# Routed tiles: one semaphore update of TensorE a slot, three PSUM banks a link, stages 3, 6 and 9 slots behind the load

## What is computed

```python
xn = (xf - mu) * jax.lax.rsqrt(var + LN_EPS) * ln_scale + ln_bias
probs = jax.nn.softmax(xn @ gate_w.T, axis=-1)
tk_probs, tk_idx = jax.lax.top_k(probs, TOP_K)          # 2 of 8 experts
tk_probs = tk_probs / (jnp.sum(tk_probs, axis=-1, keepdims=True) + EPS)
out = _swiglu(xf, sWg, sWu, sWd)                        # shared expert
for e in range(NUM_EXPERTS):
    out = out + w[:, e:e + 1] * _swiglu(xf, Wg[e], Wu[e], Wd[e])
# _swiglu(x, wg, wu, wd) = jax.nn.silu(x @ wg) * (x @ wu) @ wd
```

## Time and profile before

| | |
|---|---|
| median of 3 runs | 887.57 us (887.54 to 888.57) |
| profiled execution, its span from the first to the last instruction | 935.9 us |
| TensorE busy in it | 785.4 us, 84% |
| VectorE busy | 651.4 us, 70% |
| ScalarE busy | 573.1 us, 61% |
| GpSimd busy | 569.9 us, 61% |
| mean granted TensorE clock | 0.928 |

### The profile page before, as it was taken

One profiled execution on the slowest core, in us unless ns is written; L12 is line 12 of the kernel. 1 busy time (PEld: TensorE's weight loads), 2 busy tenths in 40 slices (PEclk: granted clock), 3 DMA queues, 4 the chain that ended last, 5 costly groups with the idle time before them and its releaser, 6 DMA issues.

```text
span 935.9 us, 37055 instructions
## 1 busy us (share of the span) xinstructions
PE 785.4 (84%) x14487; PEld 614.1 (66%) x14487; DVE 651.4 (70%) x1699; ACT 573.1 (61%) x1185; POOL 569.9 (61%) x762
## 2 busy tenths in 40 slices
PE   4888997998898888989868777899988999998890
PEld 3556676766676666667655546788767777777770
DVE  2347787888988798788787777586555555556773
ACT  4478886877887788778756554443344545545440
POOL 5455554877877787778656565357155555655562
PEclk9799998989899899889987878999999999999996
DMA  8311101220221122022112005001232222225765
GB/s 242 65 49 48 48 28 36 60 64 25 68 60 34 54 60 68 20 66 60 32 53 60 25 21 157 21 12 38 66 84 78 77 74 77 76 75 174 212 186 170
DMA packets 81446, 68.39 MB, mean 73 GB/s; under 512 B 9424, under 2 KB 71515, under 8 KB 81280
## 3 DMA queue, kind: packets, MB, share of 16 engines
q1 hardware_dynamic: 70000, 47.81, 19.4%
q0 software_dynamic: 8640, 16.93, 5.4%
q10 hardware_dynamic: 2640, 1.31, 0.5%
HBM read 42.91 MB, written 24.02 MB: 72 GB/s over the span
## 4 chain that ended last, share of the span: by engine, by line
PE 41%; DVE 26%; issue 17%; ACT 8%; SPq 4%; DMA 2%; another core or an unknown queue 1%; POOL 1%; POOLq 0%; ACTq 0%; DVEq 0%
PE pair_x L886 8%; PE bank L904 7%; PE bank L501 4%; DVE mx L1510 4%; PE pair_x L677 4%; PE pair_x L587 3%; PE bank L694 3%; DVE Ex L1514 2%; ACT Am L992 2%; DVE rot L1442 2%; DVE c_hit L1606 2%; PE bank L894 1%; PE bank L623 1%; PE pair_y L894 1%
## 5 line engine op out<-in xcount | busy, mean ns | idle before, releaser
L1405 POOL DMA_INDIRECT mixed<-f_y,f_x x142 | 139.4, 982 | 129.8 <-ACT f_y L1178 81.6
L1288 POOL DMA_INDIRECT routed<-c_row,c_idx x128 | 137.1, 1071 | 104.7 <-PE bank L694 61.2
L904 PEld LDWEIGHTS bank<-Qblk,Am 128*128 128x128 f32 x568 | 79.4, 191 | 47.4 <-issue 39.8
L904 PE MATMUL bank<-Qblk,Am 128*128 x568 | 92.5, 285 | 16.4 <-DVE Am L1816 12.2
L677 PE MATMUL pair_x<-con,Ex 128*128 128x128 f32 x512 | 77.9, 302 | 20.7 <-ACT Am L992 18.4
L1178 ACT ACTIVATE f_y<-bank,f_x 128x128 f32<-128x128 f32 x142 | 52.5, 370 | 56.8 <-PE bank L904 49.5
L992 ACT ACTIVATE Am<-pair_x 128x1024 f32<-128x1024 f32 x64 | 65.1, 1016 | 36.0 <-PE pair_x L587 27.5
L1027 ACT COPY ExT<-pair_x 128x1024 f32<-128x1024 f32 x64 | 64.5, 1008 | 34.4 <-PE pair_x L677 30.1
L1173 ACT ACTIVATE qk<-pair_x 128x256 f32<-128x256 f32 x142 | 55.5, 391 | 48.2 <-PE pair_x L886 31.0
L587 PE MATMUL pair_y<-Kblk,KQ 32*64 32x256 f32 x1024 | 82.8, 437 | 0.7 <-issue 0.7
L677 PEld LDWEIGHTS pair_x<-con,Ex 128*128 128x128 f32 x512 | 64.6, 156 | 27.4 <-issue 23.9
(11 more groups left out here) (209 smaller groups left out, 2083.0 us busy)
## 6 DMA issues: line engine op xcount, KB each, us to landing
f_x<-routed SPq DMA_DIRECT2D x142, 65.0 KB
ctxD<-in_ctx SPq DMA_DIRECT2D x32, 256.0 KB
ctxP<-in_ctx SPq DMA_DIRECT2D x16, 256.0 KB
maskB<-in_mask_BxS_if SPq DMA_DIRECT2D x16, 256.0 KB
Cblk<-mixed SPq DMA_DIRECT2D x8, 512.0 KB
Kblk<-mixed SPq DMA_DIRECT2D x8, 512.0 KB
block_out<-X SPq DMA_DIRECT2D x11, 256.0 KB
mixed<-f_y,f_x POOLq DMA_INDIRECT x142
```

The source lines that it names most:

```text
L904: ins = pe.matmul(banks[F_O[n % 2]][:, 0:D], f_hT[:, u % 3, c * P:(c + 1) * P], wdn[:, bass.ds(e, 1), c, :].rearrange("p o d -> p (o d)"), ...
L1288: pool.indirect_dma_start(routed[:, :], bass.IndirectOffsetOnAxis(ap=c_idx[:, d % ROW_SLOTS, t, n:n + 1], axis=0), c_row[:, d % ROW_SLOTS, ...
L1405: pool.indirect_dma_start(mixed[:, :], bass.IndirectOffsetOnAxis(ap=f_x[:, u, D + 1:D + 2].bitcast(I32), axis=0), f_y[:, u, :], None, boun ...
```

## The change

TensorE makes one update of one semaphore, `f_slot`, with the last matmul of each slot. ScalarE and VectorE wait for it once at the start of their slot, in place of four waits for four semaphores. The up product of a tile comes 3 slots behind its transpose (was 2), its hidden transpose 6 (was 4), its down product 9 (was 6), and LAG is 9. Each kind of PSUM result but one has three banks: the transposed tile n shares its bank with the output of tile n-9, in other columns; the hidden transpose keeps two. Since ScalarE and VectorE mustn't read one bank at once, `tile_low` now waits for `tile_end` of the same slot (`f_yd`), and comes last in VectorE's slot. SBUF rings have 4 places (were 3), the load ring 18 (was 15), in another room. The mixed sums of part 0 start 3 slots later. Four semaphores of the setup are one, with the values 1 to 4.

```diff
-UNROLL = 15
+UNROLL = 18
 EARLY_SUM, SUM_EVERY = PART_FIRST[1] + UNROLL - 1, 3
+LOAD_STEPS = max(TILE_MAX, EARLY_SUM + SUM_EVERY * (EARLY - 1) + 1)
-LAG = 6
+UP_BACK, TURN_BACK, LAG = 3, 6, 9
-E_RING = 6
+E_RING = 10
+F_RING = 4
+SET_WEIGHTS, SET_GATE, SET_BIAS, SET_TABLE = 1, 2, 3, 4
-        F_UP, F_HT, F_X, F_O = (0, 1), (3, 4), (2, 6), (5, 7)
+        F_UP, F_XO, F_HT = (0, 1, 2), (4, 5, 6), (3, 7)
...
@@ SyncE
-            for n in range(UNROLL, TILE_MAX):
+            for n in range(UNROLL, LOAD_STEPS):
...
-                load_tile(n)
+                if n < TILE_MAX:
+                    load_tile(n)
...
@@ TensorE
+            def tile_T(n, t, u):
                 pe.wait_ge(f_in[u], 16 * t + 16)
-                if n >= 2:
-                    pe.wait_ge(S["f_xTl"], n - 1)
-                pe.transpose(banks[F_X[n % 2]][:, 0:P], f_x[:, u, 0:D], ident).then_inc(S["f_xT_ps"], 1)
+                if n >= 3:
+                    pe.wait_ge(S["f_xTl"], n - 2)
+                return pe.transpose(banks[F_XO[n % 3]][:, 0:P], f_x[:, u, 0:D], ident)
...
+            def tile_up(n, e):
                 pe.wait_ge(S["f_xTl"], n + 1)
-                if n >= 2:
-                    pe.wait_ge(S["f_hd"], n - 1)
+                if n >= 3:
+                    pe.wait_ge(S["f_hd"], n - 2)
...
+            def tile_down(n, e):
+                pe.wait_ge(S["f_hTd"], n + 1)
+                if n >= 3:
+                    pe.wait_ge(S["f_yd"], n - 2)
...
+            def hidden_T(n):
+                pe.wait_ge(S["f_hd"], n + 1)
+                if n >= 2:
+                    pe.wait_ge(S["f_hTd"], n - 1)
...
             def slot(t, u):
+                n = t * UNROLL + u
+                if n < TILE_MAX:
+                    ins = tile_T(n, t, u)
+                if 0 <= n - UP_BACK < TILE_MAX:
+                    ins = tile_up(n - UP_BACK, expert_of(n - UP_BACK))
+                if 0 <= n - 1 < TILE_MAX:
+                    load_expert(n - 1)
+                if 0 <= n - LAG < TILE_MAX:
+                    ins = tile_down(n - LAG, expert_of(n - LAG))
+                if 0 <= n - TURN_BACK < TILE_MAX:
+                    ins = hidden_T(n - TURN_BACK)
+                ins.then_inc(S["f_slot"], 1)
...
@@ ScalarE
             def slot(t, u):
+                act.wait_ge(S["f_slot"], n + 1)
+                if n < TILE_MAX:
+                    tile_T_evac(n)
+                if 0 <= n - UP_BACK < TILE_MAX:
+                    tile_silu(n - UP_BACK)
+                if 0 <= n - LAG < TILE_MAX:
+                    tile_end(n - LAG)
...
@@ VectorE
+            def tile_low(n):
                 dve.wait_ge(S["f_xTd"], n + 1)
+                if n >= LAG:
+                    dve.wait_ge(S["f_yd"], n - LAG + 1)
...
             def slot(t, u):
+                n = t * UNROLL + u
+                dve.wait_ge(S["f_slot"], n + 1)
+                if 0 <= n - TURN_BACK < TILE_MAX:
+                    hidden_evac(n - TURN_BACK)
+                if 0 <= n - UP_BACK < TILE_MAX:
+                    hidden(n - UP_BACK)
+                if n < TILE_MAX:
+                    tile_low(n)
```

More of the change, by code:

```diff
@@ L449, in _ @@
                     store(i - 3)
-            for i in range((TILE_MAX - 1 - EARLY_SUM) // SUM_EVERY - 2, EARLY):
+            for i in range((LOAD_STEPS - 1 - EARLY_SUM) // SUM_EVERY - 2, EARLY):
                 store(i)
@@ L898, in tile_down @@
-            def tile_down(t, u, e):
-                n = t * UNROLL + u
-                pe.wait_ge(S["f_hTd"], n + 1)
-                if n >= 2:
-                    pe.wait_ge(S["f_yd"], n - 1)
-                for c in range(CH):
-                    ins = pe.matmul(banks[F_O[n % 2]][:, 0:D], f_hT[:, u % 3, c * P:(c + 1) * P],
+                return ins
+            def tile_down(n, e):
+                pe.wait_ge(S["f_hTd"], n + 1)
+                if n >= 3:
+                    pe.wait_ge(S["f_yd"], n - 2)
+                for c in range(CH):
+                    ins = pe.matmul(banks[F_XO[n % 3]][:, P:P + D], f_hT[:, n % F_RING, c * P:(c + 1) * P],
@@ new lines, in hidden_T @@
+            def hidden_T(n):
+                pe.wait_ge(S["f_hd"], n + 1)
+                if n >= 2:
+                    pe.wait_ge(S["f_hTd"], n - 1)
+                for c in range(CH):
+                    ins = pe.transpose(banks[F_HT[n % 2]][:, c * P:(c + 1) * P],
+                                       f_h[:, n % F_RING, c * P:(c + 1) * P], ident)
+                return ins
+            def slot(t, u):
+                n = t * UNROLL + u
[10 more added lines that the diff above has]
+                ins.then_inc(S["f_slot"], 1)
@@ L1162, in _, with tile_T_evac, tile_silu, tile_end @@
             act.wait_ge(S["s_ac"], GROUPS)
[L1164 to L1184 removed]
+            def tile_T_evac(n):
+                act.copy(f_xT_hi[:, n % F_RING, :], banks[F_XO[n % 3]][:, 0:P]).then_inc(S["f_xTd"], 1)
+            def tile_silu(n):
+                act.activation(f_sg[:, n % F_RING, :], banks[F_UP[n % 3]][:, 0:INTER], ACT.Silu).then_inc(S["f_si"], 1)
+            def tile_end(n):
+                u = n % UNROLL
+                act.activation(f_y[:, u, :], banks[F_XO[n % 3]][:, P:P + D], ACT.Copy, scale=f_x[:, u, D:D + 1])\
+                    .then_inc(S["f_yd"], 1)
+            def slot(t, u):
+                n = t * UNROLL + u
+                act.wait_ge(S["f_slot"], n + 1)
[5 more added lines that the diff above has]
+                    tile_end(n - LAG)
             routed_slots(slot)
@@ L1830, in slot @@
             def slot(t, u):
-                for stage, back in ((tile_low, 0), (hidden_evac, 5), (hidden, 2)):
-                    tile = tile_of(t, u, back)
-                    if tile:
-                        stage(*tile)
-                i, rest = divmod(t * UNROLL + u - EARLY_SUM + 1, SUM_EVERY)
+                n = t * UNROLL + u
[6 more added lines that the diff above has]
+                    tile_low(n)
+                i, rest = divmod(n - EARLY_SUM + 1, SUM_EVERY)
                 if i in range(EARLY) and rest < TOP:
```

100 lines of the change are left out of this document (29 added, 71 removed).

## The result

The changed kernel takes 900.19 us (median of 4 runs, 898.75 to 903.04); the kernel before, beside it, 888.07 us (887.54 to 889.93). The ratio is 1.0133, interval 1.0091 to 1.0176: slower by 12.1 us. The forecast was 889.0, the range 855 to 891, slower by over 0.2% with a chance of 0.26.

The account below looks back on a forecast made before the run. TensorE's own work, 1.46 us a slot, was taken as the routed stage's floor, with late releases likelier than not from recording. 0 - 2.5 (start) + 3.9 (drain) = +1.4 on 887.57 gave 889.0; own range 886.6 to 891.3, 8-in-10 range 855 to 891.

Parts of the forecast that it names:

- TensorE has one more wait a slot: 0: Routed stage: hidden_T's added wait for f_hTd is for something two slots old, so it costs 0.
- The drain, +3.9: End of routed stage: nine slots behind, more scatters queue on GpSimd after the last transpose; +3.9 us, bounds +2.5 to +3.9.
- The start, -2.5: Start of routed stage: with UNROLL 18, 18 loads go ahead of the pads, shortening TensorE's stop; -2.5 us, ends -1.5 and -3.5.
- the clock: After the stop for the pads: a longer stop can drop TensorE's clock, but both kernels have one; 0, at worst +1.3 us.
- the 34.6 us: Routed stage, tiles 18 to 141: 123 slots took 214.8 us against 180.2 at 1.465 each; the difference was called lost.
- Late releases made by recording: Routed stage: TensorE's late semaphores belong to the recording, so hiding them gains nothing in the timed median; chance 0.58.
- Three slots of slack hide late releases, -32 in such a trace: Routed stage: slack of 1.7 us hides releases 1.4 late; -32 us in a traced execution, between -34.6 and 0.
- the rival of real late releases: Routed stage: late releases occur in timed runs too, giving 855.6 us, or 860 to 885 if partly real; chances 0.25 and 0.10.
- Each update costs TensorE time: Rival, TensorE's slots: 426 fewer updates save at most 4.3 us, giving 884.7, or 877.8 by the skill; chance 0.02.
- Mixed sums behind tile_low, and the setup: 0: VectorE keeps up with mixed_sum queued behind tile_low's new wait, and merging four setup semaphores costs nothing; 0 each.

Follow-up runs that it names:

- b_wait: Kernel before with one more TensorE wait a slot, ahead of the hidden transpose, for a semaphore set in the setup: 895.79 us beside 889.75, ratio 1.0105.
- a_one_4: Changed kernel without the one added wait of TensorE's slot (hidden_T's for f_hTd; tile_down's reaches one tile further): 891.62 us beside 887.90, ratio 1.0048.
- b0_again: Kernel before, unedited, recorded a second time, on a chip where it takes about 888: 887.95 us with recording on, beside a median of 889.75.
- a0_again: Changed kernel, unedited, on a chip where the kernel before takes about 935: 951.68 us beside 933.06, ratio 1.0171.
- a_wait2: Changed kernel with two more TensorE waits a slot in hidden_T, for things long done: 917.13 us beside 887.90, ratio 1.0338.
- a_246_3: Third run of the changed kernel with stages 2, 4, 6, load ring 15 and fewer TensorE waits: 923.62 us beside 935.27 of the kernel before, ratio 0.9855.
- a_246: Changed kernel with stages 2, 4, 6, load ring 15 and fewer TensorE waits, first run: 925.84 us beside 935.56 of the kernel before, ratio 0.9887.
- a_one_again: Changed kernel with one TensorE wait a slot less, where the kernel before takes about 935: 954.21 us beside 933.06, ratio 1.0237.

## Why the prediction was wrong, step by step

**"TensorE has one more wait a slot: 0" is the step that failed.** It asked only whether the thing waited for is there in time. It always is. But a wait is also an instruction in TensorE's list, and the list with three semaphore instructions just kept up with the arrays. The fourth costs 0.06 us a slot in b_wait and 0.09 in the changed kernel: b_wait makes it in the old kernel (+6.0 us by the medians, 1.0105 by the ratio), a_one_4 takes it out of the new (8.4 of 12.1). The starts back to back in the earlier trace rows are those of a kernel where the list still fitted: they exclude that overhead is paid now, not that more of it would be.

**The rest of the sum.** With that wait gone the new kernel takes 891.62, +3.7 on the same chip, where the sum had +1.4 and its range -1.0 to +3.7: the upper end, since the drain came and the gain at the start didn't.

**The drain, +3.9: right.** From transpose of tile 141 to the last scatters, kernel before (b0_again) and after:

```profile
858.14 0.33 PE L870 MATMUL bank<-con,f_x 128*128 128x128 f32 x1
...
869.01 0.97 POOL L1405 DMA_INDIRECT mixed<-f_y,f_x  x1 [0.30 <-issue]
871.48 0.34 SPq L421 DMA_DIRECT2D Kblk<-mixed  x1
```

```profile
866.28 0.27 PE L873 MATMUL bank<-con,f_x 128*128 128x128 f32 x1
...
880.03 0.97 POOL L1413 DMA_INDIRECT mixed<-f_y,f_x  x1 [0.30 <-issue]
881.30 0.97 POOL L1413 DMA_INDIRECT mixed<-f_y,f_x  x1 [0.30 <-issue]
883.68 0.34 SPq L424 DMA_DIRECT2D Kblk<-mixed  x1
```

The last scatter ends 11.8 us behind the transpose before and 16.0 after (forecast 11.4 and 15.3): +4.2. Scatters come every 1.27 to 1.28 as forecast.

**The start, -2.5: mis-sized, about 0.** SyncE in the changed kernel, and TensorE's transpose of tile 18, to be laid beside the earlier trace rows:

```profile
636.80 19.29 SPq L418 DMA_DIRECT2D f_x<-routed  x18
656.85 8.28 SPq L411 DMA_DIRECT2D routed<-pad  x8
665.88 33.18 SPq L418 DMA_DIRECT2D f_x<-routed  x26
```

```profile
667.79 0.33 PE L873 MATMUL bank<-con,f_x 128*128 128x128 f32 x1 [4.32 <-DMA f_x<-routed]
```

Counted from the first transpose, load 18 is issued 3.5 us later than load 15 was in b0_again (3.3 forecast), and tile 18 is transposed at 25.3 instead of 28.3. But the two slots behind the stop of 4.3 us take 3.00 and 1.82, at a low clock. In b0_again the two slots behind its own stop (2.94 and 1.87) are over ahead of tile 18. So at tile 21 the gain is 1.0 us, and the clock costs both kernels the same, as forecast. In a_one_4 nothing is left of it at tile 141: 214.64 us from tile 0, as 214.59 in b0_again.

In the last 30 slots both lose something that the prediction doesn't have: 5.9 us over 30 slots of 1.467 in b0_again, 6.7 in a_one_4. Again it is TensorE's list. Its load of the expert's number takes 0.30 us up to tile 111, and then 0.49 in the mean in b0_again and 0.52 in a_one_4, at most 1.12 and 1.30. These add up to 5.6 and 6.6 us. Why the load takes longer there isn't shown. So of the 34.6 us that the prediction had as lost to late releases, b0_again, which has none, loses 6.1 over the same 123 slots.

**Late releases made by recording: the mechanism was wrong, and the number for the median right by the luck of the chip.** The recorded execution on a chip with 888 has none, and takes as long as the others there (887.95 beside 889.75). On a chip with 935 the traced execution of a0_again takes 951.27, the others 949.38 to 952.32. So the recording adds nothing on either sort, and the 48.3 us between the first trace and the median are the difference between two sorts of chips, as far as its span tells. The Trainium skill, "NOTIFIC — the notification-queue block", section 3, has it that back-pressure of the recording path can stall an engine; no run here shows such a stall, and b0_again shows that recording can be free of it.

**Three slots of slack hide late releases, -32 in such a trace: wrong.** The changed kernel is 18.6 us slower there (a0_again). The term was priced by ScalarE's idle time, 1.4 and at most 1.9 in the earlier trace rows, against a slack of 1.7. But ScalarE had been busy for part of the time: from the end of the matmul the same trace has up to 2.4, which 1.7 doesn't cover. So the rival of real late releases, 855.6, was mis-priced too: where they are real, the kernel loses.

**Each update costs TensorE time: no.** Four updates in b0_again and one in a_one_4, 1.467 in both. The 26.3 ns for each that the Trainium skill, "TensorE: Matmul & The Clock Gate", part 3, has for the tail behind the last matmul don't appear where one slot follows another.

**Mixed sums behind tile_low, and the setup: 0, borne out.** In a_one_4 no slot from tile 21 to 121 takes over 1.62 us. In the stretch of the mixed sums, from tile 112 on, TensorE waits for VectorE once, 0.5 us. Tile 0 comes at 642.46 after the change and at 643.55 before.

## What to carry to other kernels

Ahead of adding a wait, even one that is always met, look at how near the engine's list of instructions is to its arrays: a gap "issue" at the weight loads in every slot is a sign that the list is the bound, though the arrays look 99% busy. It is no proof and no measure: a_wait2, with slots 0.1 us longer than the changed kernel's, has 27.0 us of it against 25.7, and a_246_3, whose slots are held by a wait for `tile_low`, has 89 such gaps with one semaphore instruction a slot. Test it with one wait that never waits; if the slot grows, take waits out that others cover. And don't explain a slow trace by the recording before the same kernel has been recorded again on another chip. A change that gains on a chip of one sort may lose on the other: a_246 gains 9 to 12 us where the kernel before takes 935, and hasn't been on one with 888.

## What the runs showed of the hardware

- A semaphore instruction in TensorE's list takes 0.051 us by the records, and a wait 0.06 of a slot once the list is the bound (b_wait; two waits 0.13 in a_wait2). None of it shows as a wait: from 700 to 850 the arrays of the changed kernel count as busy for 148.78 of 150 us, those of b0_again for 147.75, though there are 950 matmul instructions in the one and 991 in the other (windows, after and b0_again):

```profile
700.00:850.00 150.00, 148.78 (x950) 119.90 (x950) 106.31 (x299) 76.70 (x284) 92.63 (x96) 1.00 0.42 115
```

```profile
700.00:850.00 150.00, 147.75 (x991) 131.58 (x990) 111.49 (x316) 96.74 (x298) 96.97 (x100) 1.00 0.47 132
```

- TensorE's load of one number to a register takes 0.30 us in the middle of the stage, and up to 1.12 (b0_again) and 1.39 (after) in its last 30 slots, where the loads of `mixed` and the stores run too (DMA share 0.73 to 0.88 in b0_again from 808 to 858, 0.47 from 700 to 850).
- On chips with 935 semaphores of TensorE arrive up to 2.8 us (a_one_again) behind the modelled end of the matmul when undisturbed slots take 1.47 to 1.55 us, and seldom at 1.6; in the traces on chips with 888 they are read 0.04 us behind it. The Trainium skill, "Perfetto Trace Analysis", section "Per-instruction lifecycle: what the profiler-reported window actually captures", says that this end is computed and that the update follows once PSUM has acknowledged; so the trace can't say whether the matmul or its semaphore is late.
- Behind the stop of 4.3 us the granted clock was 0.57, near the 1.2 GHz level (it had been 1.00 ahead of the stop), and the matmuls of the next slot took 0.63 and 0.78 us in place of 0.39 and 0.48. Changed kernel, window 668 to 672, and TensorE in order of time:

```profile
668.00:672.00 4.00, 4.00 (x15) 3.45 (x15) 0.81 (x3) 0.81 (x3) 0.00 (x0) 0.57 0.30 66
```

```profile
668.08 0.78 PE L888 MATMUL pair_x<-wup_hi,f_xT_hi 128*128 x1
668.66 0.63 PE L888 MATMUL pair_x<-wup_hi,f_xT_lo 128*128 x1
```
